# Convolution with group norm: a 4-byte write per partition into the output, issued ahead of the first load

## The chip, the cores and the metric

The kernel runs on one core of one Trainium2 chip. The metric is device time in microseconds, from the runs of the whole kernel on the chip; lower is better.

## The reference

The input `x` is 8 images of 32 channels and 128x128 pixels, in float32, with a 3x3 weight of 32x32 channels and a bias of 32. The reference is

```
def _gn(v, G=16, eps=1e-5):            # per image and group of 2 channels
    g = v.reshape(B_, G, C_ // G, H_, W_)
    m = jnp.mean(g, axis=(2, 3, 4)); s = jnp.var(g, axis=(2, 3, 4))
    return ((g - m) / jnp.sqrt(s + eps)).reshape(v.shape)
x = x + _L0_conv_ref(_gn(x), L0_conv_weight, L0_conv_bias, 1, 1)
```

The convolution is written with a 256x256 FFT, and the window cut out of the result is shifted. Only the image part from row and column 62 on reaches the output as a true convolution sum, so a quarter of each image gets convolution plus bias and the rest gets the bias alone. The input is 16.8 MB and the output as much again.

## The kernel before

**Layout.** The host arranges `x` as 4 pairs of images. A pair is a tensor of 128 partitions (4 pixel phases times 32 channels), 2 images, 64 rows and 64 columns; so one image is 16 KiB per partition, 2 MiB in all, and one pair is 4 MiB. All of it stays in SBUF (`pairs`, `xts`), and the results are written in place over `x` and stored from there. There is one output tensor `out` of the same layout.

**Loads.** SyncE (SP) issues all loads of `x` at the start, in lines 185 to 194: image 0 in two halves of 1 MiB, then images 1, 2 and 3 of 2 MiB each, then pairs 2 and 3 of 4 MiB each. They are 7 DMAs on one queue, through the helper `load` (lines 180 to 183), and each has a semaphore of its own. ScalarE issues one more DMA, the 62 KB of weights and bias (line 190). Each DMA of 128 partitions runs on 16 DMA engines.

**Work.** For each image VectorE sums it (L283), ScalarE sums its squares (L303), TensorE adds over the channels of a group (L318), and a short chain on ScalarE and VectorE makes the scale and shift (L330 to L347). ScalarE writes the normalized quarter `g` (L373, L362 for the last image). TensorE multiplies it in 3 pieces of 4 products, each 2 instructions per product in the trace (L412). VectorE adds the result and the bias to `x` (L428), and GpSimd adds the bias to the rest of the image (L394). PE's instructions are emitted as a loop over pairs (`emit_loop`).

**Stores.** SyncE issues the stores in program order as the results are ready (line 437, called at lines 506, 508, 532, 533 and 536): `out[0]` and `out[1]` as whole pairs of 4 MiB, then images 4, 5 and 6 of 2 MiB each, then the last image in pieces: 189 KB from GpSimd (line 531), 800 KB and 3 KB from SyncE, and last the 1056 KB that hold the convolution of the last image (line 536). All of SyncE's stores count on one semaphore, `stored`. SyncE waits at the end for it and clears all semaphores (lines 543 to 553).

Of the kernel before, what the change touches and what calls it, by code (L numbers as in the profile page):

```python
# [29 lines left out]
F32 = mybir.dt.float32  # L30
# [3 lines left out]
P = 128  # L34
# [119 lines left out]
def conv_preact_kernel(nc: bass.Bass, x: bass.AP, wb: bass.AP, out: bass.AP):  # L154
# [10 lines left out]
    def sbuf(name, *shape):  # L165
        return nc.alloc_sbuf_tensor(name, list(shape), F32).ap()
# [4 lines left out]
    put = Queues(nc)  # L171

    pairs = [sbuf(f"x{pair}", P, 2, H, W) for pair in range(NPAIR)]
# [6 lines left out]
    def load(to, of, by="sp"):  # L180
        name = f"load{len(put.sems)}"
        put.semaphore(name)
        return put(by, lambda e: e.dma_start(to, of), adds=name)  # L183

    loaded[0] = []
    for half in range(2):
        rows = slice(half * H // 2, (half + 1) * H // 2)
# [26 lines left out]
    for step, base in ((-1, 0), (1, 1)):  # L214
# [3 lines left out]
                out=pair, in_=pair, pattern=[[2 * step, P // 2], [0, 2]], base=base,  # L218
# [36 lines left out]
    def take_first(img, *needs):  # L255

        first_ok[img] = put(
            "pool", lambda e: e.tensor_copy(sums[(img - 1) % 2][:, 2:3], xts[img][:, 0, 0:1]),  # L258
            *rows_in(img, 1), *needs, *([group_ok[img - 3]] if img > 3 else []), mark=True,
        )  # L260
# [50 lines left out]
    def group(img, part=0):  # L311

        last = len(parts(img)) - 1
        of = to_sum(img, part)
        ok = put(
            "pe",
            lambda e: e.matmul(  # L318
                ps_ms[:, 0 : of.shape[1]], avg, of, start=(part == 0), stop=(part == last)
            ),  # L320
            *(sums_ok[img][part :: last + 1]), *([first_ok[img + 1]] if img and img + 1 < B else []),
            avg_ok, *means_read.get(img - 1, ()), mark=part == last,
        )
        if part == last:
            group_ok[img] = ok

    def take_std(img):
        square_ok = put(
            "act",
            lambda e: e.activation(squares[img], ps_ms[:, 0:1], AF.Square, bias=origins[img]),  # L330
            group_ok[img], origin_ok[img], mark=True,
        )
        var_ok = put(
            "dve",
            lambda e: e.tensor_scalar(variances[img], ps_ms[:, 1:2], squares[img], None, op0=ALU.subtract),  # L335
            square_ok, mark=True,
        )

        std_ok = put(
            "act",  # L340
            lambda e: e.activation(stds[img], variances[img], AF.Sqrt, bias=eps, scale=float(FFT * FFT)),  # L341
            var_ok, mark=True,
        )
        rstd_ok = put("dve", lambda e: e.reciprocal(rstds[img][:, 0:1], stds[img]), std_ok, mark=True)  # L344
        shift_ok = put(
            "dve",
            lambda e: e.tensor_scalar(  # L347
                rstds[img][:, 1:2], ps_ms[:, 0:1], rstds[img][:, 0:1], -1.0, op0=ALU.mult, op1=ALU.mult
            ),
            rstd_ok, mark=True,  # L350
        )
        means_read[img] = (shift_ok,)

    def normalize(img):

        xt, g, rstd = xts[img], gs[img % 2], rstds[img]
        normal[img] = []
        if img + 1 == B:

            ok = put(  # L360
                "act",
                lambda e: e.activation(  # L362
                    g, xt[:, LO:H, LO:W], AF.Identity, bias=rstd[:, 1:2], scale=rstd[:, 0:1]
                ),
                *means_read[img], *rows_in(img, H), *conv_ok.get(img - 2, ()), mark=3,
            )
            normal[img] = [put.ahead(ok, 2), put.ahead(ok, 1)]
            sums_ok[B] = [ok, put("dve", lambda e: e.tensor_copy(idle, eps), eps_ok, mark=True)]
            return
        for rows in (slice(0, ROWS + 1), slice(ROWS + 1, N)) if img == 0 else (slice(0, N),):  # L370
            ok = put(
                "act",
                lambda e: e.activation(  # L373
                    g[:, rows, :], xt[:, LO + rows.start : LO + rows.stop, LO:W], AF.Identity,
                    bias=rstd[:, 1:2], scale=rstd[:, 0:1],
                ),
                *means_read[img], *rows_in(img, H), *conv_ok.get(img - 2, ()), mark=rows.start == 0,
            )
            if ok:
                normal[img].append(ok)  # L380
        pilot_back(img + 1)
        normal[img].append(origin_ok[img + 1])

    def add_bias(*imgs):

        xt = pairs[imgs[0] // 2] if len(imgs) == 2 else xts[imgs[0]].unsqueeze(1)
        low = xt[:, :, N:H, :].rearrange("p b h w -> p b (h w)")
        right = xt[:, :, 0:N, N:W]
        free = [token for img in imgs for token in (*normal[img], *sums_ok[img])]  # L390
        free += [bias_ok] + ([warm_ok] if 0 in imgs else [])
        marks = (len(imgs) == 2 or imgs[0] >= B - 2, True)
        tokens = [
            put("pool", lambda e: e.tensor_scalar(part, part, 1.0, bias_sb, op0=ALU.mult, op1=ALU.add), *free, mark=mark)  # L394
            for part, mark in zip((low, right), marks)
        ]
        for img in imgs:
            biased[img] = [token for token in tokens if token]

    def multiply(img, n, products=range(4)):  # L400
        g = gs[img % 2]

        ps = pss[img % 2][:, n, 0 : ROWS * N].rearrange("p (r w) -> p r w", w=N)
        for k in products:
            dr, dc = k // 2, k % 2

            rows = min(ROWS, N - dr - n * ROWS)
            top = n * ROWS + dr
            needs = [normal[img][min(n, 1)]] + added.get(img - 2, [])
            ok = put(  # L410
                "pe",
                lambda e, k=k, dc=dc, rows=rows, top=top: e.matmul(  # L412
                    ps[:, 0:rows, 0 : N - dc], w_sb[:, k * P : (k + 1) * P],
                    g[:, top : top + rows, dc:N],
                    start=(k == 0), stop=(k == 3),
                ),
                *needs, mark=k == 3,
            )
        if ok:
            conv_ok[img] = [ok]  # L420

    def add(img, first, last):

        part = xts[img][:, first * ROWS : last * ROWS, 0:N].rearrange("p (n r) w -> p n r w", r=ROWS)
        ps = pss[img % 2][:, first:last, 0 : ROWS * N].rearrange("p n (r w) -> p n r w", w=N)
        ok = put(
            "dve",
            lambda e: e.scalar_tensor_tensor(part, in0=ps, scalar=bias_sb, in1=part, op0=ALU.add, op1=ALU.add),  # L428
            *conv_ok[img], bias_ok, mark=True,
        )  # L430
        added.setdefault(img, []).append(ok)
# [4 lines left out]
    def store(to, of, *needs, by="sp"):  # L436
        return put(by, lambda e: e.dma_start(to, of), *needs, adds="moved" if by == "pool" else "stored")

    def finished(*imgs):
        return [token for img in imgs for token in (*biased[img], *added[img])]  # L440
# [28 lines left out]
    for q in range(4):  # L469
# [22 lines left out]
        adds="moved",  # L492
# [7 lines left out]
    for img in range(B):  # L500
        multiply(img, 0)
        multiply(img, 1, range(3))
        if img:
            add(img - 1, 0, NCHUNK)
            if img == 2 or img == 4:
                store(out[img // 2 - 1], pairs[img // 2 - 1], *finished(img - 2, img - 1))
            elif img > 4:
                store(out[(img - 1) // 2, :, (img - 1) % 2], xts[img - 1], *finished(img - 1))
        group(img + 1)
        multiply(img, 1, range(3, 4))  # L510
        if img + 1 < B:
            take_std(img + 1)
            normalize(img + 1)
            if img < B - 4:
                take_first(img + 3)
            if img == B - 5:
                take_first(img + 4)
            if img in (0, 2):
                add_bias(img, img + 1)
            elif img > 2:  # L520
                add_bias(img + 1)
        multiply(img, 2)
        if img + 2 < B:
            sum_squares(img + 2)
            sum_up(img + 2)
# [68 lines left out]
```

How the kernel before makes its waits and increments, by code:

```python
    def __call__(self, name, emit, *needs, mark=False, adds=None):  # L68
# [9 lines left out]
            self.done[name] += 1  # L78
            return {**seen, name: self.done[name]}, name
        waits = {}
        for token, of in needs:
            if seen.get(of, 0) < token[of]:
                waits[of] = max(waits.get(of, 0), token[of])
        for token, of in needs:
            self._learn(name, token)
        waits = list(waits.items())
        for of, value in waits[:-1]:
            engine.wait_ge(self.sems[of], value)
        op = emit(engine)
        if waits:
            of, value = waits[-1]
# [2 lines left out]
            of, by = adds, LANDED  # L94
        elif mark:
            of, by = name, int(mark)
        else:
            return None
        op.then_inc(self.sems[of], by)
        self.done[of] += by
        return {**seen, of: self.done[of]}, of
# [7 lines left out]
    def emit_loop(self, times, steps):  # L109
# [26 lines left out]
            at[of] = first  # L136
            engine.reg_mov(values[of], at[of])
        begin = dict(at)
        with engine.Fori(0, times):
            for place in range(size):
                emit, _, mark = rounds[0][place]
                for of, value in plan[place].items():
                    if value != at[of]:
                        engine.reg_add(values[of], values[of], value - at[of])
                        at[of] = value
                    engine.wait_ge(self.sems[of], values[of])
                op = emit(engine)
                if mark:
                    op.then_inc(self.sems["pe"], 1)
```

## Time and profile before

| What | Value |
|---|---|
| Time, median of 3 runs | 83.39 us (83.38 to 83.54) |
| Profiled execution: span from the first to the last instruction | 82.0 us |
| Instructions | 686 |
| PE busy | 66.8 us, 81% |
| VectorE busy | 50.2 us, 61% |
| ScalarE busy | 47.9 us, 58% |
| GpSimd busy | 31.6 us, 39% |
| DMA packets | 2164, 33.62 MB, mean 410 GB/s |
| Share of 16 DMA engines' span: SyncE's queue q1 | 96.3% |
| the other queues q0 (GpSimd) and q10 (ScalarE) | 0.6% and 0.3% |
| Longest wait of SyncE's last instruction for a store | 4.2 us |

The profile gives the span of one execution; no device time of that same execution is listed beside it. The median of the runs is 1.4 us above the span, and this is what lies around the span. The share of a DMA queue is the time that its packets took, divided by 16 engines' time. A stretch can show over 100%, because a packet is counted whole in the stretch in which it starts. L412 is line 412 of the kernel.

### The profile page before, as it was taken

How to read it: one execution, taken by the hardware profiler on the slowest of the kernel's cores; microseconds unless marked ns; L12 is line 12 of the kernel's file. 1: busy time of each engine (PE TensorE's matmuls, PEld its weight loads, DVE VectorE, ACT ScalarE, POOL GpSimd, SP SyncE). 2: the span in 40 equal slices, each digit the busy share in tenths (PEclk: the TensorE clock that was granted, in tenths of full speed). 3: DMA queues.
4: the chain of work that ended last, by engine and by line, in shares of the span. 5: the costliest groups of instructions: out<-in, count | busy, mean ns of one | idle time of the engine just before them, and what ended most of it. 6: DMA issues, size and time to landing. Idle time of an engine off the chain costs nothing.

```text
span 82.0 us, 686 instructions
## 1 busy us (share of the span) xinstructions
PE 66.8 (81%) x222; PEld 41.3 (50%) x222; DVE 50.2 (61%) x43; ACT 47.9 (58%) x53; POOL 31.6 (39%) x43
## 2 busy tenths in 40 slices
PE   0009974999999999999999999999999999993000
PEld 0005433566666666666666656666666666660000
DVE  0009936960899499769949995996899324006000
ACT  3307967981699299569947974994798260000000
POOL 6876000004069900106992930490085029400000
PEclk9999998579999999999999999999999999999965
DMA  2899999999979979979959889989979999999995
GB/s 40 299 415 443 463 415 423 447 407 423 551 304 511 479 320 479 511 336 431 511 256 511 383 383 511 447 352 479 463 336 423 423 431 439 431 423 419 397 430 239
DMA packets 2164, 33.62 MB, mean 410 GB/s; under 512 B 296, under 2 KB 330, under 8 KB 500
## 3 DMA queue, kind: packets, MB, share of 16 engines
q1 hardware_dynamic: 2020, 33.36, 96.3%
q0 software_dynamic: 96, 0.19, 0.6%
q10 hardware_dynamic: 48, 0.06, 0.3%
HBM read 16.84 MB, written 16.78 MB: 410 GB/s over the span
## 4 chain that ended last, share of the span: by engine, by line
PE 74%; DMA 14%; DVE 2%; SPq 1%; issue 0%
PE ps L412 73%; DMA x<-x_dram 14%; DVE x L428 2%; PE ps_m L318 1%; SPq L183 1%; PE ps_w L265 0%
## 5 line engine op out<-in xcount | busy, mean ns | idle before, releaser
L412 PE MATMUL ps<-g,w_sb 128*128 128x363 f32 (+1 forms) x192 | 60.7, 473 | 0.1
L412 PEld LDWEIGHTS ps<-g,w_sb 128*128 128x128 f32 x192 | 36.1, 194 | 20.0 <-ACT origin L292 1.4
L283 DVE TENSOR_REDUCE sums<-x 128x1 f32<-128x4096 f32 x7 | 30.9, 4411 | 0.6 <-DMA x<-x_dram 0.6
L394 POOL TENSOR_SCALAR x<-x,bias_sb 128x1984 f32<-128x1984 f32 (+3 forms) x12 | 23.2, 1945 | 18.9 <-ACT origin L292 14.6
L303 ACT ACTIVATE unused<-x,origin 128x4096 f32<-128x4096 f32 (+1 forms) x9 | 30.0, 3330 | 0.3
L428 DVE SCALAR_TENSOR_TENSOR x<-ps,bias_sb,x 128x1089 f32<-128x1089 f32 (+2 forms) x9 | 10.9, 1220 | 7.7 <-PE ps L412 7.7
L373 ACT ACTIVATE g<-x,rstd 128x1089 f32<-128x1089 f32 (+2 forms) x8 | 9.4, 1190 | 3.4 <-DVE rstd L347 3.4
L283 DVE TENSOR_REDUCE first_sums<-x 128x1 f32<-128x2048 f32 x2 | 4.6, 2286 | 6.2 <-DMA x<-x_dram 6.2
L258 POOL COPY sums<-x 128x1 f32<-128x1 f32 x6 | 1.0, 186 | 18.2 <-DMA x<-x_dram 18.2
L335 DVE TENSOR_SCALAR var<-ps_m,square 128x1 f32<-128x1 f32 x8 | 1.8, 219 | 8.2 <-ACT square L330 8.2
L265 PE MATMUL ps_w<-x,avg 128*128 128x1 f32 x4 | 0.9, 304 | 7.1 <-POOL w_sb L476 6.1
L330 ACT ACTIVATE square<-ps_m,origin 128x1 f32<-128x1 f32 x8 | 2.1, 261 | 7.3 <-PE ps_m L318 7.3
L447 PE MATMUL ps<-x,avg 128*128 128x512 f32 x6 | 4.9, 942 | 0.0
L265 PEld LDWEIGHTS ps_w<-x,avg 128*128 128x128 f32 x4 | 0.8, 248 | 7.9 <-POOL w_sb L476 6.1
L318 PEld LDWEIGHTS ps_m<-sums,avg 128*128 128x128 f32 x16 | 2.8, 188 | 2.2 <-DVE x L428 1.0
L341 ACT ACTIVATE std<-var,eps 128x1 f32<-128x1 f32 x8 | 2.4, 294 | 2.3 <-DVE var L335 2.3
L344 DVE RECIPROCAL rstd<-std 128x1 f32<-128x1 f32 x8 | 1.3, 164 | 2.9 <-ACT std L341 2.9
L292 ACT ACTIVATE origin<-ps_w 128x1 f32<-128x1 f32 x2 | 0.3, 160 | 4.0 <-PE ps_w L265 4.0
L476 POOL COPY w_sb<-wb_sb 32x128 f32<-32x128 f32 (+1 forms) x8 | 2.5, 340 | 0.0
L318 PE MATMUL ps_m<-sums,avg 128*128 128x3 f32 x16 | 2.3, 214 | 0.0
L447 PEld LDWEIGHTS ps<-x,avg 128*128 128x128 f32 x6 | 1.5, 287 | 1.0 <-issue 1.0
L237 ACT ACT_TABLE_LOAD x1 | 1.3, 1283 | 1.2 <-PEq L579 1.2
(21 smaller groups left out, 13.3 us busy)
## 6 DMA issues: line engine op xcount, KB each, us to landing
x<-x_dram SPq DMA_DIRECT2D x2, 4096.0 KB, 34.3
out_dram<-x SPq DMA_DIRECT2D x2, 4096.0 KB
x<-x_dram SPq DMA_DIRECT2D x3, 2048.0 KB, 16.0
out_dram<-x SPq DMA_DIRECT2D x3, 2048.0 KB
x<-x_dram SPq DMA_DIRECT2D x2, 1024.0 KB, 6.2
out_dram<-x SPq DMA_DIRECT2D x1, 1056.0 KB
out_dram<-x SPq DMA_DIRECT2D x1, 800.0 KB
out_dram<-x POOLq DMA_DIRECT2D x1, 189.0 KB, 7.7
```

Source lines behind the costliest of these rows:

```text
L283: lambda e: e.tensor_reduce(to_sum(img, k)[:, 0:1], piece, mybir.AxisListType.X, ALU.add),
L303: lambda e: e.activation(unused[:, rows.start * W : rows.stop * W], piece, AF.Square, bias=origins[img], accum_out=to_sum(img, k)[:, 1:2],),
L318: lambda e: e.matmul(ps_ms[:, 0 : of.shape[1]], avg, of, start=(part == 0), stop=(part == last)),
L330: lambda e: e.activation(squares[img], ps_ms[:, 0:1], AF.Square, bias=origins[img]),
L335: lambda e: e.tensor_scalar(variances[img], ps_ms[:, 1:2], squares[img], None, op0=ALU.subtract),
L341: lambda e: e.activation(stds[img], variances[img], AF.Sqrt, bias=eps, scale=float(FFT * FFT)),
L373: lambda e: e.activation(g[:, rows, :], xt[:, LO + rows.start : LO + rows.stop, LO:W], AF.Identity, bias=rstd[:, 1:2], scale=rstd[:, 0:1],),
L394: put("pool", lambda e: e.tensor_scalar(part, part, 1.0, bias_sb, op0=ALU.mult, op1=ALU.add), *free, mark=mark)
L412: lambda e, k=k, dc=dc, rows=rows, top=top: e.matmul(ps[:, 0:rows, 0 : N - dc], w_sb[:, k * P : (k + 1) * P], g[:, top : top + rows, dc:N] ...
L428: lambda e: e.scalar_tensor_tensor(part, in0=ps, scalar=bias_sb, in1=part, op0=ALU.add, op1=ALU.add),
L447: "pe", lambda e: e.matmul(pss[1][:, 0, :], avg, piece, start=True, stop=True),
L476: lambda e: e.tensor_copy(w5[to, :, dc, :, c.start * C : c.stop * C], taps[:, 1 - rin : 5 - rin, b, :].rearrange("p (dr r) b o -> p dr r ( ...
```

## The change

```
--- before.py
+++ after.py
@@ -182,6 +182,10 @@
         put.semaphore(name)
         return put(by, lambda e: e.dma_start(to, of), adds=name)
 
+    put.semaphore("early")
+    early = put(
+        "sp", lambda e: e.dma_start(out[0, :, 0, 0, 0:1], nc.const_aps.tensor(0.0, [P, 1], F32), allow_slow_non_contiguous=True), adds="early"
+    )
     loaded[0] = []
     for half in range(2):
         rows = slice(half * H // 2, (half + 1) * H // 2)
@@ -503,7 +507,9 @@
         if img:
             add(img - 1, 0, NCHUNK)
             if img == 2 or img == 4:
-                store(out[img // 2 - 1], pairs[img // 2 - 1], *finished(img - 2, img - 1))
+                store(
+                    out[img // 2 - 1], pairs[img // 2 - 1], *([early] if img == 2 else []), *finished(img - 2, img - 1)
+                )
             elif img > 4:
                 store(out[(img - 1) // 2, :, (img - 1) % 2], xts[img - 1], *finished(img - 1))
```

SyncE gets one more DMA, its first: from the tile of zeros in SBUF, 4 bytes in each of 128 partitions, into the first element of each partition's row of `out[0]`. It has a semaphore of its own, `early`. The first store, of the whole of `out[0]`, writes the same bytes later with the result and waits for `early` besides what it waited for. No other instruction is changed.

## Rows read from the trace of the kernel before

**Rows 1.** The page: DMA share and GB/s in 40 equal slices of the span.
```profile
DMA  2899999999979979979959889989979999999995
GB/s 40 299 415 443 463 415 423 447 407 423 551 304 511 479 320 479 511 336 431 511 256 511 383 383 511 447 352 479 463 336 423 423 431 439 431 423 419 397 430 239
```

**Rows 2.** The windows: stretch, its length, busy us of each engine, PEclk, DMA share, GB/s.
```profile
3.00:81.00 78.00, 66.83 (x222) 41.29 (x222) 50.22 (x43) 46.40 (x51) 29.42 (x35) 0.96 1.01 427
76.00:78.00 2.00, 0.00 (x0) 0.00 (x0) 0.06 (x1) 0.00 (x0) 0.00 (x0) 1.00 0.95 393
78.00:80.00 2.00, 0.00 (x0) 0.00 (x0) 0.00 (x0) 0.00 (x0) 0.00 (x0) 0.67 1.02 428
80.00:81.00 1.00, 0.00 (x0) 0.00 (x0) 0.00 (x0) 0.00 (x0) 0.00 (x0) 0.50 0.98 414
```

**Rows 3.** The chain that ended last, in order of time: start us, us, what.
```profile
1.73 11.62 DMA x<-x_dram
13.34 0.04 issue
13.39 0.38 PE ps_w L265 x2
...
71.55 3.01 PE ps L412 x10
74.56 0.02 issue
74.58 1.48 DVE x L428 x2
```

**Rows 4.** SyncE's DMA issues of the last, first and second store: start us, us, what.
```profile
76.09 0.35 SPq L437 DMA_DIRECT2D out_dram<-x  x1
34.37 0.35 SPq L437 DMA_DIRECT2D out_dram<-x  x1
49.06 0.34 SPq L437 DMA_DIRECT2D out_dram<-x  x1
```

**Rows 5.** DMA packets that start between 76.09 us and the end.
```profile
DMA packets 350, 2.08 MB, mean 346 GB/s; under 512 B 66, under 2 KB 68, under 8 KB 217
```

**Rows 6.** SyncE's first two DMA issues, in order of time.
```profile
0.81 0.39 SPq L183 DMA_DIRECT2D x<-x_dram  x1
1.25 0.42 SPq L183 DMA_DIRECT2D x<-x_dram  x1
```

**Rows 7.** The windows at the start, as in rows 2.
```profile
1.40:1.80 0.40, 0.00 (x0) 0.00 (x0) 0.00 (x0) 0.40 (x1) 0.40 (x1) 1.00 0.00 0
1.80:2.20 0.40, 0.00 (x0) 0.00 (x0) 0.00 (x0) 0.40 (x1) 0.33 (x2) 1.00 1.54 246
```

**Rows 8.** Packets of 1.8:2.2, then 2.2:3 (two queues), then 4:5 us.
```profile
q1 hardware_dynamic: 12, 0.10, 154.4%
...
q1 hardware_dynamic: 11, 0.09, 42.3%
q10 hardware_dynamic: 13, 0.03, 15.4%
...
q1 hardware_dynamic: 53, 0.43, 103.0%
```

**Rows 9.** Packets of 28:40, 39.2:40.2, 40:41 and 50:52.4 us.
```profile
DMA packets 176, 5.24 MB, mean 437 GB/s; under 512 B 16, under 2 KB 16, under 8 KB 16
q1 hardware_dynamic: 176, 5.24, 101.5%
...
q1 hardware_dynamic: 16, 0.52, 121.7%
...
q1 hardware_dynamic: 16, 0.52, 166.4%
...
DMA packets 48, 1.05 MB, mean 437 GB/s; under 512 B 16, under 2 KB 16, under 8 KB 16
q1 hardware_dynamic: 48, 1.05, 101.6%
```

**Rows 10.** Timeline: GpSimd at the start and with the weights; PE after them.
```profile
0.32 0.09 POOL L579 MEMSET const-float32-0.0<- 128x1 f32 x1 [0.32 <-issue]
4.46 0.18 POOL L472 COPY bias_sb<-wb_sb 32x1 f32<-32x1 f32 x1 [0.46 <-DMA wb_sb<-wb_dram]
7.00 0.63 POOL L476 COPY w_sb<-wb_sb 32x256 f32<-32x256 f32 x2
11.28 1.10 PE L447 MATMUL ps<-x,avg 128*128 128x512 f32 x2
```

More of the change, by code:

```diff
@@ L183, in load @@
         return put(by, lambda e: e.dma_start(to, of), adds=name)
+    put.semaphore("early")
+    early = put(
+        "sp", lambda e: e.dma_start(out[0, :, 0, 0, 0:1], nc.const_aps.tensor(0.0, [P, 1], F32), allow_slow_non_contiguous=True), adds="early"
+    )
     loaded[0] = []
@@ L505, in conv_preact_kernel @@
             if img == 2 or img == 4:
-                store(out[img // 2 - 1], pairs[img // 2 - 1], *finished(img - 2, img - 1))
+                store(
+                    out[img // 2 - 1], pairs[img // 2 - 1], *([early] if img == 2 else []), *finished(img - 2, img - 1)
+                )
             elif img > 4:
```

## The prediction

> **What bounds the kernel now.** I read the page's slices first: the DMA row is full from the second slice to the last but one [rows 1]. The windows say the same in one number: from 3 to 81 us the 16 DMA engines are 101% busy and move 427 GB/s, while PE is busy 67 of 78 us [rows 2]. Next the chain of waits. It names the first loads, then PE without a break, then the last addition, which ends at 76.06 us [rows 3]. The span ends at 82.0, though, and its last 6 us belong to the stores. The last store is issued at 76.09 [rows 4]. From then on 2.08 MB are moved [rows 5], of which this store is 1056 KB, that is 1.08 MB; so about 1.0 MB stood in the queue ahead of it, worth 2.3 us at 427 GB/s. The engines come to it at about 78.4 us. A DMA needs some 1.0 us from its issue to its first packet (0.81 to 1.8 us) [rows 6, 7], so it was ready at 77.1: the computation has a slack of about 1.3 us. The DMA engines set the end, from the first packet to the last, and the reader should keep two questions: when does the stream start, and where does it stall?
>
> **It stalls once.** In the steady stream a packet of 32 KB takes 1.22 us: 101.5% of 16 engines in 12 us is 194.9 us for 160 packets, the other 16 being the 4-byte ends of a load [rows 9]. The 16 packets that start from 39.2 to 40.2 us take 1.22 us each. The 16 that start from 40 to 41 take 26.6 us together, 1.66 us each, so each engine loses 0.45 us there. By the bytes (16.8 MB in, at 427 GB/s, from 2.8 us) this is where the loads end and the first store begins, though that store was issued at 34.37 already [rows 4]. At the turn from the first store to the second, from 50 to 52.4 us, 32 such packets take 39.0 us, again 1.22 us each: no stall. Nor is there one at the turn of two loads inside 28 to 40 us. So something is paid on the first write to the output alone.
>
> **The added DMA at the start.** SyncE's first issue takes 0.39 us and the next follows 0.44 us after it [rows 6]. One more issue in front moves all 7 loads by 0.44 us; each waits for nothing and they fill the queue, so the stream is moved as a whole. The zero tile is set at 0.32 us [rows 10], ahead of the 0.81 at which SyncE starts, so the new DMA waits for nothing. Its packets are 128 of 4 bytes, 8 on each engine. They can start at about 1.8 us, where the first load's start now, and the load's come at 1.8 + 0.44. Do they fit in these 0.44 us? If the first write to the output costs what it costs at 40 us, 0.45 on each engine, they just don't, with the 8 packets themselves on top. No row shows a 4-byte write to DRAM. I take 0.01 us each, as for any packet with next to no data (the 16 short ends in the 50 to 52.4 us stretch leave no mark on the time of the others), so 0.07. The sum is 0.52 us instead of 0.44.
>
> The bounds of this term are wide. **Below:** the stream starts badly now. The first 12 packets, of 8 KB, take 9.9 us, 0.82 us each, against 0.31 for one in the stretch from 4 to 5 us [rows 8]. Up to 3.0 us only 0.22 MB are moved; at 0.43 MB a us this is 0.51 us of work in 1.16, so 0.65 us are lost. Should the small DMA take over all of that loss, the term is 0.44 - 0.65 = -0.2 us. **Above:** the small writes and the loads' slow first packets come after each other and neither is hidden, so 0.44 + 0.51 = 0.95 us. I take 0.52, the value of the parts that rows price; the loads' own slow first packets are then paid as now.
>
> The Trainium skill has a rule against this change: on its page "DMA: Bandwidth & Descriptors", in the table Specifications, a transfer needs at least 512 bytes for full rate, and below that the engine reads, modifies and writes back. With the 0.2 us that its section "Latency and other measured facts" gives for an HBM access, 8 such writes one after another would be an estimated 1.6 us on each engine, and the sum would be a kernel 1.2 us slower instead of 0.1. No row of this trace has a short write to DRAM, and the rival for it is below.
>
> **The gain at the first store.** If the stall comes with the first write to the output and what it sets up stays for 38 us, it is gone: 0.45 us on each engine, all of it on the path, since the engines never run dry. Below it is 0. Above, the packets of the slowest engine may lose more than the mean, say twice, 0.9; I take 0.45.
>
> **The added wait.** SyncE waits for `early` ahead of the first store. Nothing queues behind it but stores, and `early` will have been reached some 30 us before 34.37. A second wait is one more instruction on SyncE; even at a whole issue, 0.4 us, the first store has 6 to 7 us until the stream comes to it, and the second store, issued at 49.06, has 2 to 3. I cost it at nothing.
>
> **What moves with it.** The weights come on ScalarE's queue and may stand behind the new packets. GpSimd waits for them at 4.46 us, and its last copy ends at 7.63. PE needs it at 11.28 [rows 10], so up to 3 us are covered. The loads of images 0 and 1 start the computation [rows 3], which therefore also comes 0.5 us later, while the stream comes 0.5 later and 0.45 earlier again. The slack of 1.3 us shrinks to about 0.9. The end stays with the DMA.
>
> **Sum.** Span 82.0 + 0.52 - 0.45 = 82.07, and with the 1.4 us around it, 83.46 by the median of 83.39. I say 83.45.
>
> **Rivals.**
> *The slow start is taken over (faster).* The first packets are slow because the engines themselves, or the path to DRAM, are used for the first time, not because of what they read. For it: the 13 packets of the weights that start between 2.2 and 3 us belong to another tensor, read for the first time, and take 15.4% of 16 engines in 0.8 us, 0.15 us each, far less than the 0.82 of the loads' first [rows 8]. Then the small DMA pays while SyncE still issues the first load. Against: it must not itself be longer than 0.44 us. The term at the start is -0.1 to 0.2 and the gain stays: 82.9 to 83.2, middle 83.05.
>
> *The stall is the turn (slower).* The 0.45 us at 40 us come from each engine turning from reading DRAM to writing it, with the last loads still under way, or what the early write sets up is lost in the 38 us of loads. For it: the slow packets are the last of the loads, not the first of the store. Then nothing is gained and the start is paid: 83.39 + 0.44 to 0.95, middle 83.9. It decides as soon as the packets that start at 40 to 41 us (0.5 later in the new trace) still take over 1.5 us each. Here the change does not do what it was put in for.
>
> *The short writes are slow (slower by far).* If each of the 8 writes on an engine costs 0.45 us and none overlaps, the loads start 3.6 us after 1.8 and not 0.44: 83.39 + 3.6 - 0.45 = 86.5, or some 85 with half of that. The page's rule named above points to this one. I hold it unlikely, since the steady stream shows the engines working on several packets at a time: full rate with 16 packets of 4 bytes among the others.
>
> **How the numbers follow.** A difference of 0.2%, 0.17 us, is about what a measurement of this kernel can tell from none. My forecast, with both terms nearly equal, has 0.37: of it 0.24 lie within 0.17 us, 0.11 are slower, as the start can cost up to 0.3 more, and 0.02 faster. The taken-over start has 0.28, of which 0.27 faster. The turn has 0.27, nearly all slower. The slow short writes have 0.05. The remaining 0.03 go half to faster and half to same or slower. In sum faster 0.30, same 0.27, slower 0.43. The forecast's own range is 83.2 to 83.75. The range for 8 in 10 takes in the middle of the taken-over start and all but the top of the turn, 82.95 to 84.1.
>
> **What would show it.** The first load issued at about 1.25 us, its first packets at about 2.3, and a full stream from about 3.3 to 3.4 instead of 3.0; a landing of image 1, and the start of PE's chain, at 13.9 instead of 13.39; 32 KB packets of 1.22 us throughout the stretch at 40 to 41.5 us; a last store issued at 76.6; an end at 82.1. I am wrong on the start if PE's chain begins before 13.6 or after 14.2, and on the gain if some 16 packets near 41 us still take over 1.5 us.

## The result, and the profile of the changed kernel

The changed kernel took 84.31 us in the median of 4 runs (84.02 to 84.69), against 83.44 us for the kernel before on the same chip: a ratio of 1.012, with a 95% interval of 1.0095 to 1.0145. It is slower by 0.9 us by the medians and by 1.0 us by the ratio, which is worked out from the single runs. The forecast was 83.45, with a range up to 84.1. Two repeats further down gave ratios of 1.0066 and 1.0146, so the size moves, the sign does not. All ratios here leave out executions in the chip's slower state.

The span of the profiled execution is 83.5 us instead of 82.0. Its own time was 84.69, the longest of the four. The page first: slices, span, and SyncE's queue.

```profile
span 83.5 us, 687 instructions
DMA  1899999999999999998969989998989999999992
GB/s 24 187 412 452 440 440 416 440 424 432 487 401 487 440 408 408 487 424 361 455 283 503 455 345 455 487 424 345 503 369 416 440 424 448 400 448 391 415 440 97
q1 hardware_dynamic: 2164, 33.36, 95.1%
```

There are 144 packets more on q1 than before: 128 writes and 16 completions. The DMA engines are as full as in [rows 1], and of the first slices it is the second that is poorer: 187 GB/s instead of 299. The last slice is thinner as well, 97 instead of 239; the end comes below.

The timeline of the start shows the added issue and what it moved (start us, us, engine, line, operation); the line of PE is from the chain of waits, where PE waits for image 1.

```profile
0.81 0.38 SPq L187 DMA_DIRECT2D out_dram<-const-float32-0.0  x1
1.25 3.71 SPq L183 DMA_DIRECT2D x<-x_dram  x7
7.01 2.29 DVE L287 TENSOR_REDUCE first_sums<-x 128x1 f32<-128x2048 f32 x1 [7.01 <-DMA x<-x_dram]
14.37 4.42 DVE L287 TENSOR_REDUCE sums<-x 128x1 f32<-128x4096 f32 x1 [0.59 <-DMA x<-x_dram]
...
14.39 0.38 PE ps_w L269 x2
```

VectorE's same two lines in the kernel before:

```profile
5.99 2.29 DVE L283 TENSOR_REDUCE first_sums<-x 128x1 f32<-128x2048 f32 x1 [5.99 <-DMA x<-x_dram]
13.37 4.42 DVE L283 TENSOR_REDUCE sums<-x 128x1 f32<-128x4096 f32 x1 [0.62 <-DMA x<-x_dram]
```

The first load is issued at 1.25 us, 0.44 us later than in [rows 6], as forecast. VectorE starts on the first half of image 0 at 7.01 instead of 5.99 us, and on image 1 at 14.37 instead of 13.37. A load has landed when the slowest of its 16 engines has, so that one is 1.0 us later, not 0.52. PE's chain begins at 14.39 instead of 13.39, above the 14.2 that the prediction named as its sign of being wrong on the start. The windows of the same stretch (stretch, length, busy us of each engine, PEclk, DMA share, GB/s), then the packets that start from 1.6 to 1.84 us:

```profile
1.80:2.20 0.40, 0.00 (x0) 0.00 (x0) 0.00 (x0) 0.40 (x1) 0.33 (x2) 1.00 0.54 159
2.20:2.60 0.40, 0.00 (x0) 0.00 (x0) 0.00 (x0) 0.39 (x2) 0.40 (x1) 1.00 1.62 164
2.60:3.00 0.40, 0.00 (x0) 0.00 (x0) 0.00 (x0) 0.14 (x1) 0.32 (x2) 1.00 0.68 102
3.00:4.00 1.00, 0.00 (x0) 0.00 (x0) 0.00 (x0) 0.00 (x0) 0.92 (x4) 1.00 0.58 213
2.00:12.00 10.00, 4.40 (x8) 2.28 (x8) 4.57 (x2) 4.98 (x7) 4.78 (x16) 1.00 0.98 380
```
```profile
DMA packets 106, 0.00 MB, mean 2 GB/s; under 512 B 106, under 2 KB 106, under 8 KB 106
q1 hardware_dynamic: 106, 0.00, 23.4%
```

The short packets are there and gone at once: 106 of them take 23.4% of 16 engines in 0.24 us, 8.5 ns each. The weights come next, and the loads' first packets start at 2.3 us. Then the slow start comes all the same, later: only 213 GB/s from 3 to 4 us, where the kernel before had this:

```profile
3.00:4.00 1.00, 0.00 (x0) 0.00 (x0) 0.00 (x0) 0.00 (x0) 0.92 (x3) 1.00 1.05 431
```

The first 16 packets of the loads took 0.80 and 0.85 us each in two profiles of the kernel before, and 1.00, 0.85 and 0.75 in three of the changed one. The slow packets were not taken over, and in this first profile they were slower still.

Last, the stretch of the first store. From 38 to 44 us only packets of 32 KB and the short ends of a load start, so the time that the packets took beyond 1.218 us each, the time of one in the steady stream [rows 9], is the stall. First the kernel before, then the changed one:

```profile
DMA packets 95, 2.59 MB, mean 431 GB/s; under 512 B 16, under 2 KB 16, under 8 KB 16
q1 hardware_dynamic: 95, 2.59, 107.6%
```
```profile
DMA packets 82, 2.20 MB, mean 366 GB/s; under 512 B 15, under 2 KB 15, under 8 KB 15
q1 hardware_dynamic: 82, 2.20, 95.4%
```

Before: 79 long packets, 107.6% of 96 us of engine time is 103.3 us, 7.1 us too much, 0.44 us per engine. After: 67 long packets, 95.4% is 91.6 us, 10.0 us too much, 0.62 us per engine. The stall that was to go has grown.

The end, in windows:

```profile
81.00:82.00 1.00, 0.00 (x0) 0.00 (x0) 0.00 (x0) 0.00 (x0) 0.00 (x0) 0.50 0.82 346
82.00:83.00 1.00, 0.00 (x0) 0.00 (x0) 0.00 (x0) 0.00 (x0) 0.00 (x0) 0.50 0.08 34
```

The kernel before:

```profile
81.00:82.00 1.00, 0.00 (x0) 0.00 (x0) 0.00 (x0) 0.00 (x0) 0.00 (x0) 0.50 0.17 68
```

So the engines finish 0.65 + 0.08, some 0.75 us later on average. But of the packets with data only four start after 82 us, and the very last packet starts at 83.06 instead of 81.61: the span ends by the slowest engine, 1.5 us later.

### The profile page after: what moved, and what is told of

Read it like the earlier page. It is cut to its first block, busy times and chain, and to the rows that moved or that the text cites. A ratio compares the mean times of both kernels' runs of the same rounds, so it can differ in the third digit from the quotient of the medians.

```text
span 83.5 us, 687 instructions
## 1 busy us (share of the span) xinstructions
PE 66.8 (80%) x222; PEld 41.3 (49%) x222; DVE 50.2 (60%) x43; ACT 47.9 (57%) x53; POOL 31.5 (38%) x43
## 4 chain that ended last, share of the span: by engine, by line
PE 73%; DMA 15%; DVE 2%; SPq 1%; issue 0%
PE ps L416 72%; DMA x<-x_dram 15%; DVE x L432 2%; PE ps_m L322 1%; SPq L183 1%; PE ps_w L269 0%; SPq L187 0%
```

## The experiments

Two measures stand beside the time. **Lateness** is how much later than in the first profile of the kernel before the trace's packets have moved so many MB in all, a mean over the engines. **Stall** is the one just read, per engine from 38 to 44 us. Each kernel with an added DMA also has the wait of the first store for it, unless said. Ratios are to the kernel before, with their 95% intervals. The last kernel of the table moves 0.26 MB more, and its lateness counts them as moved; at 17 MB in all it is not yet past its stall.

| Kernel | Time, us | Ratio | Late at 1 MB | at 15 MB | at 17 MB | Stall, us |
|---|---|---|---|---|---|---|
| before, two profiles | | | 0; 0.01 | 0; 0.00 | 0; -0.06 | 0.44; 0.38 |
| the change | 84.31 | 1.012 (1.0095-1.0145) | 0.71 | 0.56 | 0.74 | 0.62 |
| the change, 2nd | 83.91 | 1.0066 (1.0041-1.0092) | 0.33 | 0.19 | 0.46 | 0.72 |
| the change, 3rd | 84.49 | 1.0146 (1.007-1.0222) | 0.33 | 0.20 | 0.55 | 0.81 |
| into SBUF | 84.14 | 1.0089 (1.0058-1.0119) | 0.70 | 0.58 | 0.93 | 0.79 |
| a read instead | 83.89 | 1.0075 (1.0035-1.0114) | 0.33 | 0.19 | 0.59 | 0.85 |
| the same read, no wait | 84.23 | 1.0112 (1.0091-1.0133) | 0.28 | 0.14 | 0.55 | 0.81 |
| 16 partitions | 83.80 | 1.0056 (1.0036-1.0075) | 0.37 | 0.23 | 0.41 | 0.63 |
| two DMAs of 16 | 84.28 | 1.012 (1.0081-1.0159) | 0.73 | 0.59 | 1.00 | 0.86 |
| by ScalarE, behind the weights | 83.46 | 1.0022 (0.9998-1.0047) | -0.06 | -0.05 | 0.08 | 0.58 |
| by SyncE, behind the first load | 83.40 | 1.0011 (0.9979-1.0043) | -0.06 | -0.03 | 0.07 | 0.53 |
| 16 partitions at 28 us | 83.57 | 1.0031 (1.001-1.0051) | -0.07 | -0.09 | 0.17 | 0.69 |
| 2 KB in 16 partitions at 14 us | 83.60 | 1.0043 (1.0008-1.0077) | -0.01 | -0.03 | 0.14 | 0.61 |
| 2 KB in 128 partitions at 14 us | 84.12 | 1.0089 (1.0057-1.0121) | 0.02 | 0.01 | 0.01 | 0.56 |

**Is it the issue, or the write?** First the target was taken away.

```
+    touched = sbuf("touched", P, 1)
-        "sp", lambda e: e.dma_start(out[0, :, 0, 0, 0:1], nc.const_aps.tensor(0.0, [P, 1], F32), ...
+        "sp", lambda e: e.dma_start(touched, nc.const_aps.tensor(0.0, [P, 1], F32), ...
```

> The added DMA stays SyncE's first, with 128 packets of 4 bytes, but its target is a scratch tile in SBUF: nothing is written to the output early. Theory W (about half of the 0.9 us is the issue, 0.44 us, and the rest comes from writes to DRAM scattered over 4 MB ahead of the first reads): 83.44 + 0.4 to 0.5 = 83.9, PE's chain of waits for image 1 ending near 13.85. Rival D (any DMA of 128 packets in front costs it all, by the issue and the making of its packets): 84.3 as with the change, image 1 at 14.35. Rival N (DMAs into SBUF are free, all is the write): 83.4.

84.14 us. Nothing is written to DRAM early, and the kernel loses as much as with the change: rival D of the expectation. Its issue took 0.52 us and the next 0.69, though, longer than the 0.38 and 0.42 with the other targets, so that the loads' first packet started at 2.70 us instead of 2.3. Its 0.70 us of lateness is thus not that of one plain issue. Next, a read from the loads' own rows in the same place, `e.dma_start(touched, x[0, :, 0, 0, 0:1], ...)`:

> The added DMA reads 4 bytes per partition of the first load's own rows from DRAM into a scratch tile, and writes nothing to the output early. Theory W in its form that places in DRAM touched for the first time are slow: the touches are of the very rows that the load needs, so the slow start is moved into the issue time of 0.44 us: 83.4 to 83.9, first 8 KB packets under 0.8 us each. Rival D: 84.3. If only writes hurt: 83.9.

83.89 us, a loss of 0.6 with no write at all, and the stream is 0.33 us late at 1 MB. Touching the rows that the load needs did not make its start better. Then the change with one write per engine, `out[0, 0:16, 0, 0, 0:1]`:

> The change with 16 partitions instead of 128: one 4-byte write on each DMA engine, same issue on SyncE. If the writes to DRAM cost by their number (theory W, seen so far as 0.4 to 0.6 us later landings with the change than with a read in the same place), little more than the issue is left: ratio 1.005 to 1.0075, 83.8, first half of image 0 landed near 6.4 us. If any first touch of the output costs the same (rival T): 84.2 to 84.3, landed near 7.0. If the issue costs nothing by itself: 83.4.

83.80 us, late by 0.37 us at 1 MB. And two such DMAs, on partitions 0 to 15 and 16 to 31:

> Two DMAs of 16 partitions, one 4-byte packet per engine each, on SyncE ahead of the loads; the first store waits for both. If the price of one DMA in front is its issue on SyncE (0.44 us between issues), the second costs the same again: stream 0.7 to 0.8 us late at 8 MB instead of 0.25 to 0.35 with one, time 83.4 + 0.8 to 0.9 = 84.25. Rival (what costs is that a write to DRAM goes first at all, once): 83.8 as with one.

84.28 us, late by 0.73 us: the second costs 0.36, as much as the first. By the bytes moved in all, each DMA in front of the first load costs some 0.35 us, by its place in SyncE's program, and a read of 128 rows costs no more than a write of 16. The chain of waits of this kernel shows where it is paid, two issues before that of the first load:

```profile
0.81 0.38 SPq L187
...
1.25 0.41 SPq L191
...
1.71 0.41 SPq L183
```

Against the number of writes: the change itself, in its second and third profile, was 0.33 us late like the kernel with 16. The 0.71 of the first profile was not seen again for it. So my theory of costly scattered writes, which that profile had suggested, is not borne out by the mean of the bytes.

> The change once more, for a second profile. All theories: start of the stream 0.6 to 0.75 us late, slow packets ahead of the first store as before or worse, median 84.2 to 84.4. If the first profile's late end (the last engine 1.45 us late where the mean of the bytes was 0.79 us late) is scatter between engines, it is smaller here, 0.8 to 1.2.

83.91 us.

> The change once more. Its median so far is 84.3 and 83.9 in two jobs. If its start costs one issue and the rest of the first profile was scatter: the stream 0.3 to 0.4 us late at 1 MB and a median of 83.8 to 84.1. If the 128 short writes usually cost the start more: 0.6 to 0.75 us late and 84.2 to 84.4.

84.49 us. By the mean the start is that of one issue both times (0.33 us), but the median of the third is above what the expectation gave for that case. The rest of its loss is in the stall, and in the last engine, which ended 1.24 and 1.18 us late in these two profiles where the mean of the bytes was 0.96 and 0.57 late.

**Where does the last engine fall behind?** Each DMA ends with a 4-byte packet on every engine, so their starts in the trace show how far the last engine is behind the mean of the 16:

| Kernel | End of the first load, us | of the sixth load | of the first store |
|---|---|---|---|
| before, two profiles | 0.26; 0.27 | 0.27; 0.26 | 0.35; 0.25 |
| the change, three profiles | 0.69; 0.34; 0.61 | 0.68; 0.33; 0.60 | 1.06; 0.24; 0.96 |
| the read, and the same without the wait | 0.43; 0.37 | 0.42; 0.35 | 0.55; 0.44 |
| 16 partitions; two DMAs of 16 | 0.16; 0.18 | 0.18; 0.19 | 0.52; 0.29 |

In the first and third profile the lag is there by the end of the first load, is carried unchanged through 27 us of loads, grows in the stall, and is what separates the last engine from the mean at the end. In the second it is small up to the first store; that one lost 0.4 us near 76 us instead, where packets of 16 KB took up to 1.00 us against 0.61. The lag at the start was smaller in each of the two kernels with 16 writes than in all five profiles with 128 writes to DRAM or reads from it, and the first half of image 0 landed 0.17 us late with 16 writes against 0.29 to 1.02 in those five. So the number of packets may cost something on the slowest engine after all. With one to three profiles a kernel this is not shown.

**Only the place.** The change's DMA was issued by ScalarE behind the weights, and then by SyncE behind its first load. The second is the change with one move:

```
     for half in range(2):
         ...
         if half == 0:
             weights_in = load(wb_sb, wb, by="act")
+            put.semaphore("early")
+            early = put("sp", lambda e: e.dma_start(out[0, :, 0, 0, 0:1], ...), adds="early")
```

> The write of the change is issued from ScalarE, behind the weights, with SyncE's queue as in the kernel before: the loads are issued at 0.81 us again. If the issue on SyncE is 0.44 us of the cost and the scattered writes the rest (theory W): 83.44 + 0.3 to 0.5, 83.85, or less if the reads are under way by then. Rival D: 83.4 to 83.5, as the issue is all there is. The stall at 40 us: 0.45 us per engine as before, since the change has left it at that too.

> The change with its DMA issued by SyncE behind the first load instead of ahead of it; nothing else is moved. If the place ahead of the first load is the loss, the stream starts on time (0 to 0.1 us late at 1 MB) and what is left is the longer stall at the first store: 83.4 + 0.1 to 0.3. If the writes and the issue cost the same wherever SyncE issues them at the start: 84.0 to 84.3.

83.46 and 83.40 us. With the same write, the same issue on SyncE and the same wait, but one place later, the ratio is 1.0011 (0.9979 to 1.0043) and nothing is late. SyncE and VectorE in the timeline of the latter:

```profile
0.81 0.39 SPq L183 DMA_DIRECT2D x<-x_dram  x1
1.26 0.42 SPq L193 DMA_DIRECT2D out_dram<-const-float32-0.0  x1
...
5.90 2.29 DVE L287 TENSOR_REDUCE first_sums<-x 128x1 f32<-128x2048 f32 x1 [5.90 <-DMA x<-x_dram]
```

The first load's 1 MB keeps the engines busy while SyncE issues the write. This shows that the loss at the start comes with the place ahead of the first load. It did not bring the gain that was the other half of the idea: its stall is 0.53.

**Does an early write prepare the first store?** It did not from 1.7 us on. Perhaps it faded, so the write was put into the main loop, on ScalarE near 28 us:

```
+            if img == 1:
+                put.semaphore("early")
+                early = put("act", lambda e: e.dma_start(out[0, :, 0, 0, 0:1], ...), adds="early")
```

> The kernel before with the same 4-byte writes issued by ScalarE after image 2 is normalized, near 29 us, some 12 us ahead of the first store's packets, and no DMA at the start. Theory Turn: the stall at 40 to 41 us stays, 0.45 to 0.8 us per engine, time 83.3 to 83.5. Rival Faded (an early write prepares the first store but does not last 38 us): the stall is gone, time 82.9.

85.13 us, ratio 1.0221 (1.0195 to 1.0246), for another reason. SyncE's queue of waits says that the first store waited for the small write, which landed 14.6 us after its issue; the store was issued at 42.58, the loads ran out, and the engines stood still:

```profile
42.58 0.35 SPq L437 DMA_DIRECT2D out_dram<-x  x1
```
```profile
42.00:43.40 1.40, 1.40 (x6) 0.87 (x5) 1.19 (x3) 0.92 (x2) 0.66 (x3) 1.00 0.00 0
```
```profile
DMA packets 305, 4.33 MB, mean 393 GB/s; under 512 B 173, under 2 KB 173, under 8 KB 173
q1 hardware_dynamic: 161, 4.33, 91.1%
q10 hardware_dynamic: 144, 0.00, 0.7%
```

The last fence holds the packets of 31 to 42 us: all 144 of ScalarE's queue lie there, 9 per engine among as many of 32 KB, so each short packet waited for a long one. The Trainium skill says so ("DMA: Bandwidth & Descriptors", Queues, rings and completion order): an engine takes turns between its queues, a packet at a time. The trace agrees: its short packets start once every 1.21 us, from 31.95 us on, and 9 turns of 1.22 us are 11 us. The other 3.6 us or more lie between the issue at 27.95 and the first packet. With 16 partitions the write landed after 6.5 us. The first store waited for it until 35.32, which was still in time:

> As the late write before (whose 8 short packets per engine went out one by one between packets of 32 KB, so that it landed only after 14.6 us and held up the first store), now with 16 partitions, one 4-byte packet per engine, issued by ScalarE near 28 us and landed by 33 us. No DMA at the start. Theory First (the slow packets ahead of the first store are paid for the first write, and what an early write sets up fades between 12 and 38 us): no packets over 1.5 us near 41 us, time 82.9 to 83.0. Theory Bulk (short writes do not prepare the first large store at all): the slow packets stay, 0.45 to 0.8 us per engine, time 83.3 to 83.5.

83.57 us, and the stall is 0.69. Nor did longer writes help, of 2 KB from the prepared weights near 14 us (`out[0, 0:128, 0, 0:8, :]` from `w_sb`, and the same for 16 partitions):

> The kernel before with one write of 2 KB per partition in 128 partitions (the prepared weights, overwritten by the first store, which waits for it), issued by ScalarE near 14 us in the midst of the loads. It costs 0.26 MB, 0.6 us of the stream. Theory First, for writes of full rate: the slow packets move to 16 to 20 us and are gone near 41 us, time 83.4 + 0.6. Rival Turn (they belong to the place where the stores take over from the loads, whatever was written before): still 0.45 to 0.8 us per engine near 41 us, time 83.4 + 0.6 to 0.9.

> The same with 16 partitions, one packet of 2 KB per engine, 33 KB in all and less than 0.1 us of the stream. Theory First: gone near 41 us, time 83.0 to 83.4. Rival Turn: still there, 83.4 to 83.6.

84.12 and 83.60 us, with stalls of 0.56 and 0.61. So an early write did not take the stall away in any of these forms: short or long, 16 partitions or 128, issued 40 to 13 us ahead. Two kernels with an early write had no stall, though. In the one with 128 writes near 28 us the store came only after the loads had run dry, so it can't tell. The other is the kernel with all writes in one place, further down: its loads and first store follow each other as before, 10 us later, and every packet ahead of the store takes 1.22 us. What makes it the exception was not tested.

**Is the stall the turn from loads to stores?** The kernel before got a second turn, by loading image 7 again into a scratch tile between the first two stores.

> The kernel before with a load of 2 MB of image 7 again, into a scratch tile that nobody reads, issued between the first and the second store: the stream turns from loads to stores twice. Theory Turn (the slow packets at 40 us come from engines that turn from loads to stores): the last 16 packets of the added load, near 56 us, are slow too, 1.3 to 1.7 times their 0.61 us. Rival First (the first write to the output costs it): they take 0.61 us, and only the turn near 42 us stalls. Total about 83.4 + 4.9 us for the 2 MB.

88.21 us in one run. At the first turn the stall is 0.49. Around the second, from 53 to 58 us:

```profile
DMA packets 128, 2.11 MB, mean 423 GB/s; under 512 B 16, under 2 KB 16, under 8 KB 16
q1 hardware_dynamic: 128, 2.11, 100.9%
```

That is 80.7 us of engine time for 2.11 MB. At 1.218 us for 32 KB (37.2 us a MB) it should be 78.5, so 0.14 us per engine: some stall, a third of the first. Then the first store was issued by ScalarE, on a queue of its own:

> The kernel before with the first store issued by ScalarE, so on a queue of its own: its packets interleave with the last loads' from 35 us on instead of following them. Theory Turn in the form that all engines at once change from loads to stores: no common stall near 41 us, the time 82.9 to 83.4 if the later landing of the last pair delays nobody. Rival First: some packets near 36 us are slow by 0.45 us per engine, and the time is 83.3 or more.

84.13 us, ratio 1.0074 (1.0045 to 1.0104). Issued at 35.62, its packets mix with the last loads', and the loads' packets just ahead of its first are slow nevertheless. From 36 to 41 us:

```profile
q1 hardware_dynamic: 38, 1.25, 73.8%
q10 hardware_dynamic: 11, 0.36, 16.7%
```

49 packets take 72.4 us instead of 59.7, 0.79 us per engine, though 1.0 MB of the loads is still to come, until 46 us. So it is not the very end of the loads that is slow, but the time ahead of the first large store. Why stays open: neither "first write" nor "turn" fits all of these runs.

**Why is the stall longer with an added DMA?** Without one it is 0.38, 0.44 and 0.49 us in three profiles, with one 0.53 to 0.86, the two kernels without a stall aside.

> The kernel before once more, for a second profile. If the larger stall of all kernels with an extra DMA (0.6 to 0.87 us per engine in the stretch of the first store) is scatter, it is above 0.55 here too; if it comes with the extra DMA, 0.40 to 0.52 as in the first profile and in the kernel with the added load.

One run: 83.14 us and 0.38. The three values of the kernels without an added DMA do not reach the others.

> The kernel with a 4-byte read per partition ahead of the loads (83.89 with its wait), where the last store waits for that read and the first store does not. Start as there, 0.33 us late. If the added wait of the first store makes the packets ahead of it slower: 0.40 to 0.50 us per engine, 0.2 to 0.35 faster than with the wait, 83.6. If the wait is free, as predicted: 0.6 to 0.87 us per engine and 83.9.

84.23 us and 0.81, against 83.89 and 0.85 for the same read with the wait: without it the stall is as long and the kernel no faster, so the wait is free, as predicted. What in the added DMA lengthens the stall stays open.

**Two on the size of the writes.** The 128 short writes were sent into 512 bytes side by side, `out[0, 0, 0, 0:2, :].rearrange("h w -> (h w)").unsqueeze(1)`:

> As the change, with 128 packets of 4 bytes from 128 partitions into the output, but into 512 bytes that lie side by side instead of one place in each row of 32 KB. Theory W (the scatter over 4 MB costs the second half): 83.9, first packets of the loads at 2.3 us with a ramp as before. Rival S (128 short writes to DRAM cost it, wherever they go): 84.3. Rival D: 84.3.

92.81 us, ratio 1.1035 (1.098 to 1.109). It fits none of the cases. The windows show loads that crawl for ten microseconds:

```profile
2.00:12.00 10.00, 0.00 (x0) 0.00 (x0) 0.00 (x0) 0.73 (x2) 1.84 (x4) 1.00 1.01 52
```

The engines count as 101% busy and move 52 GB/s. The small DMA landed 12.0 us after its issue instead of 1.8. And there is no stall ahead of the first store, from 48 to 53 us:

```profile
q1 hardware_dynamic: 82, 2.16, 100.7%
```

And 512 bytes per partition instead of 4, from a tile that VectorE sets:

> The change with 512 bytes per partition instead of 4, from a tile that VectorE sets to zero first (SyncE's first issue therefore some 0.1 to 0.3 us later). If the half of the start's delay that grows with the number of writes comes from their being under 512 bytes (read, modified, written back): the stream is 0.35 + 0.2 us late, time 83.9 to 84.0. If it comes from 128 separate writes whatever their size, or from the places they touch: 0.9 us late, time 84.4 to 84.6.

84.48 us, ratio 1.0104 (1.0038 to 1.0169): the interval holds both cases, so this says nothing. Its profile is that of the longest of its four runs, 85.73 us, and isn't used.

## Why the prediction was wrong

**What bounds the kernel** was right. The DMA engines set the end in both kernels, and whatever made the stream late came out in the time.

**The gain at the first store failed, and it is the step that turned the result.** I took 0.45 us, from "something is paid on the first write to the output alone" [rows 9]. The rows showed where the stall is, not what ends it. Instead of going, the stall went from 0.44 to 0.62, 0.72 and 0.81 us in three profiles. The term is a loss of 0.2 to 0.4, and what causes the stall stays open. Its lower bound, 0, was not low enough, because I let no case have the stall grow. The sign that the prediction named is there: near 41 us 18, 17 and 20 packets of the three profiles took over 1.5 us, against 11 in the kernel before.

**The start** was put at 0.52 us. By the bytes it was 0.33 us in two profiles and 0.71 in one. The issue in front is the right cause, shown by the second DMA (0.36 more) and by the move behind the first load (nothing). That the term exceeded the 0.44 of the issue rested on a first write at 0.45 us per engine, and no run shows such a price: with a read in its place the stream was 0.33 and 0.28 us late. The slow first packets were not taken over; the window of 3 to 4 us above shows them again, later. That rival is refuted. Its evidence also compared unlike packets: those of the weights hold 2 KB at most, the loads' first 8 KB.

**The mean was taken for the end.** I reckoned with means over 16 engines. The first half of image 0 landed 1.02, 0.32 and 0.59 us later in the three profiles, and the last engine ended 1.45, 1.24 and 1.18 us later where the mean of the bytes was 0.79, 0.96 and 0.57 late. No term stood for it. It lifts the time above 83.39 + 0.33 + 0.2 = 83.9.

**The rivals.** "The stall is the turn" had the outcome right (nothing gained, the start paid; middle 83.9, top 84.34) and the chance too low; its cause, the turn, is at best part of it. "The short writes are slow" did not happen with the change, whose packets took 8.5 ns, but a price of that order exists elsewhere: in one place of 512 bytes 128 such writes cost 9.5 us. The prediction held that rival unlikely because it read the steady stream as several packets at a time on each engine. The trace does not show that: from 12 to 38 us exactly 16 packets are under way in 93% of the time, one for each engine.

**The added wait** and what moved with it cost nothing, as predicted. **The chances** gave slower 0.43, which was the largest, beside a number in the middle that rested on two unsure terms cancelling.

## What to carry to other kernels

In this kernel, whose DMA queue never runs dry, the time from the first instruction to the first large load is on the path: a DMA ahead of it cost some 0.35 us at least, and one place behind it the same DMA cost nothing that could be measured. So in such a kernel look first at what stands ahead of the first load. A stall seen at a place is a price only once something has been shown to remove it; until then its term reaches from a loss to a gain. A mean over the engines is not the end: ask also for the last of them. And a completion that something waits for should have few packets on each engine where another queue is full of large ones (14.6 us with 8 writes on each engine, 6.5 with one).

## What was not expected of the hardware

- 128 writes of 4 bytes from 16 engines into the same 512 bytes of DRAM held up the loads behind them for some 9.5 us, an estimated 75 ns a write (9.5 us over 128); into 128 rows 32 KB apart they made the stream 0.33 us late in two of three profiles, no more than 16 writes or a read did.
- A DMA of 8 short packets per engine, issued behind full queues, landed after 14.6 us among packets of 32 KB, and after 6.5 us with one packet per engine.
- Where the last DMA engine was 0.6 to 0.7 us behind the mean of the 16 at the end of the first load, it was as far behind 27 us later, at the end of the sixth.
- Ahead of the first large store the 32 KB packets of the loads take up to 2.25 us instead of 1.22 (2.7 with the first store on ScalarE's queue), 0.4 to 0.9 us per engine, in all kernels here but two. It was absent: where the store came after the loads had run dry, and in the kernel with the writes in one place (82 packets from 48 to 53 us at 100.7%).
- A 4-byte DMA into SBUF took 0.52 us to issue, and the next issue 0.69 us, against 0.38 and 0.42 into DRAM, in one profile.
